# First attention of a two-layer kernel: VectorE's chores dealt anew over the eight head pairs, the choice of experts moved to the fifth pair, each pair's reciprocals taken within the pair

## The reference

```python
h = layernorm(x) * (1 + ca) + sa                     # per batch
q, kv = h @ w_q, h @ w_kv                            # keys and values are one tensor
q, kv = rotary(q) * scale, rotary(kv)
lkv = layernorm_per_head(kv, g, b)                   # local keys and values, windows of 128 and the one before
pkv = softmax(segments_of_16(kv) @ w_proj)           # 16 pooled keys per head
gkv = layernorm_per_head(sum(segments * pkv))
attn = softmax([q @ gkv, q @ lkv] with masks)
x = x + ga * (attn @ [gkv, lkv] @ w_out + b_out)
# then, for layer 0's experts:
h = layernorm(x) * (1 + cb) + sb
top2 = top_k(h @ router_w, 2)                        # two of four experts per token, with softmax weights
```

## Time and profile before

| what | value |
|---|---|
| median of 3 runs | 1521.95 us (1512.76 to 1534.51) |
| the profiled execution's own time | 1513.62 us |
| its span, first to last instruction | 1511.8 us |
| busy, share of the span | PE 79%, DVE 62%, PEld 61%, ACT 54%, POOL 48% |
| mean granted TensorE clock | 0.896 |
| first head pair to last of layer 0's attention | 86.09 to 551.96 us |

### The profile page before, as it was taken

One profiled execution on the slowest core, in us unless ns is written; L12 is line 12 of the kernel. 1 busy time (PEld: TensorE's weight loads), 2 busy tenths in 40 slices (PEclk: granted clock), 3 DMA queues, 4 the chain that ended last, 5 costly groups with the idle time before them and its releaser, 6 DMA issues. The chain is left out here.

```text
span 1511.8 us, 30131 instructions
## 1 busy us (share of the span) xinstructions
PE 1200.5 (79%) x9299; PEld 928.5 (61%) x9299; DVE 931.4 (62%) x2122; ACT 822.3 (54%) x2181; POOL 725.5 (48%) x750
## 2 busy tenths in 40 slices
PE   3368988989889993898899899889937887888436
PEld 1245665656656662898899889889913444444336
DVE  4687787787876533744744664764434677776633
ACT  1256777767677771676676666666612443344101
POOL 2646748567485312565566556556653323211223
PEclk8589999989998995999999999999966999899558
DMA  7500000000000003303003000000063445331145
GB/s 221 174 2 3 1 10 3 8 10 0 9 2 8 10 8 127 124 11 125 8 11 120 16 9 10 12 12 7 10 174 81 84 87 104 58 48 21 23 121 152
DMA packets 152775, 76.43 MB, mean 51 GB/s; under 512 B 99992, under 2 KB 143384, under 8 KB 152408
## 3 DMA queue, kind: packets, MB, share of 16 engines
q1 hardware_dynamic: 144696, 66.42, 16.8%
q0 software_dynamic: 3072, 6.31, 1.3%
q10 hardware_dynamic: 4896, 2.36, 0.5%
HBM read 54.77 MB, written 19.76 MB: 49 GB/s over the span
## 5 line engine op out<-in xcount | busy, mean ns | idle before, releaser
L1477 POOL TENSOR_TENSOR hl<-hid,hh 128x256 fp32r<-128x256 f32 x396 | 294.0, 744 | 218.8 <-ACT hh L1454 215.1
L1520 DVE SCALAR_TENSOR_TENSOR hid<-GU,gub,sg 128x256 f32<-128x256 f32 x396 | 190.5, 482 | 194.7 <-ACT sg L1448 123.5
L1348 PE MATMUL GU<-xh,wh 128*128 128x256 f32 x792 | 233.3, 295 | 39.4 <-DVE wl L1496 30.3
L1448 ACT ACTIVATE sg<-GU,gub 128x256 f32<-128x256 f32 x396 | 188.1, 475 | 123.6 <-PE GU L1350 121.7
L1349 PE MATMUL GU<-xl,wh 128*128 128x256 f32 x792 | 225.3, 284 | 0.0
L1350 PE MATMUL GU<-xh,wl 128*128 128x256 f32 x792 | 225.1, 284 | 0.0
L1348 PEld LDWEIGHTS GU<-xh,wh 128*128 128x128 f32 x792 | 152.1, 192 | 49.0 <-issue 27.3
L1454 ACT CAST hh<-hid 128x256 fp32r<-128x256 f32 x396 | 158.2, 399 | 25.8 <-DVE hid L1520 25.3
L1349 PEld LDWEIGHTS GU<-xl,wh 128*128 128x128 f32 x792 | 152.5, 193 | 0.0
L1350 PEld LDWEIGHTS GU<-xh,wl 128*128 128x128 f32 x792 | 152.2, 192 | 0.0
L648 ACT ACTIVATE prob<-prob,rZ 128x272 f32<-128x272 f32 (+1 forms) x256 | 98.9, 462 | 60.6 <-DVE rZ L1021 55.2
(11 more groups left out here) (312 smaller groups left out, 2842.6 us busy)
## 6 DMA issues: line engine op xcount, KB each, us to landing
raw<-in_expert_w SPq DMA_DIRECT2D x4, 2688.0 KB, 12.0
late<-in_w SPq DMA_DIRECT2D x20, 256.0 KB, 6.1
raw<-in_expert_w SPq DMA_DIRECT2D x4, 1152.0 KB, 6.1
list<-zero SPq DMA_DIRECT2D x4, 1024.0 KB, 8.6
modb<-mod_d SPq DMA_DIRECT2D x9, 384.0 KB, 4.3
early<-rel_d SPq DMA_DIRECT2D x1, 3072.0 KB, 13.1
qkv_d<-qkv SPq DMA_DIRECT2D x48, 64.0 KB
early<-in_w SPq DMA_DIRECT2D x12, 256.0 KB, 4.2
```

The source lines that it names most:

```text
L1348: pe.matmul(out, lhs[0], rhs[0], start=start, stop=False, skip_group_check=True)
L1448: act.activation(sg[:, c % BUFS], GU[c % BUFS][:, 0:TT], ACT.Silu, bias=gub[:, GATE, e * CH0 + c:e * CH0 + c + 1]).then_inc(silu, 1)
L1477: pool.tensor_tensor(hl[:, b], hid[:, b], hh[:, b].bitcast(F32), ALU.subtract).then_inc(hid_lo, 1)
L1520: dve.scalar_tensor_tensor(out=hid[:, c % BUFS], in0=GU[c % BUFS][:, TT:2 * TT], scalar=gub[:, UP, e * CH0 + c:e * CH0 + c + 1], in1=sg[:, ...
```

## The change

Nothing is computed otherwise; the same instructions run, apart from their order.

- Reciprocals of pair n move from the top of pair n+1 into pair n itself, behind the first part of that pair's chores, with the same wait on the pair's own exponentials.
- `kv_center(0)` moves from hp 7 to hp 6, `kv_center(1)` from hp 0 of the next slot to hp 7 of this one. `kv_rotate(0)` moves from hp 6 to hp 5. `kv_cosine(1)` stays in hp 6, `kv_rotate(1)` in hp 7.
- The first sum of squares moves from hp 2 to hp 1; the statistics of layernorm 2 from `residual` at hp 2 to `layernorm2` at hp 3.
- `router_rows` and `choose` move from hp 5 to hp 4, `list_places` from hp 7 to hp 6; with them PE's `router_mm` (hp 5 to 4) and `pos_mm` (hp 7 to 6) and ACT's small exponential (hp 6 to 5). The two banks' orders follow.

The diff; of the ladder that is removed only the head is shown:

```diff
--- before.py
+++ after.py
@@ -312,8 +312,8 @@
         r_step = sem("r_step"); ln2_rstd = sem("ln2_rstd"); n2_done = sem("n2_done"); h2_done = sem("h2_done")
         t_step = sem("t_step"); t_exp = sem("t_exp"); slot_out = sem("slot_out"); kv_rstd = sem("kv_rstd"); g_rstd = sem("g_rstd")
         scat = sem("scat"); count_mm = sem("count_mm"); count_out = sem("count_out")
-        bank0 = Bank(sem("a0_full"), sem("a0_drained"), "lgT:E out:L h2T:L G:E kv00:N kv10:N kT1:E kT3:E pos:L")
-        bank1 = Bank(sem("a1_full"), sem("a1_drained"), "pkT:E hT:N kv01:N router:L kv11:N gkT:E kT0:E kT2:E")
+        bank0 = Bank(sem("a0_full"), sem("a0_drained"), "lgT:E out:L h2T:L G:E kv00:N kv10:N pos:L kT1:E kT3:E")
+        bank1 = Bank(sem("a1_full"), sem("a1_drained"), "pkT:E hT:N router:L kv01:N kv11:N gkT:E kT0:E kT2:E")
         where = {}
         for b, t in ((bank0, A0), (bank1, A1)):
             for name, _ in b.order:
@@ -589,15 +589,17 @@
                         out_mm(slot, slot - 1)
                     if early and hp == 4:
                         G_mm(slot, slot + 1)
-                    if late and hp == 5:
-                        router_mm(slot, slot - 1)
                     if early and hp == 6:
                         gkT_mm(slot, slot + 1)
+                    if late and hp == 6:
+                        pos_mm(slot, slot - 1)
                     if early and hp == 7:
                         for c in (2, 3):
                             kT_mm(slot, slot + 1, np_, c)
                     if (late if hp < 2 else heads):
                         av(n - 2, slot if hp > 1 else slot - 1, bp if hp > 1 else np_, (hp - 2) % HP)
+                    if late and hp == 4:
+                        router_mm(slot, slot - 1)
                     if last:
                         pT_tr(n - 1, (hp - 1) % HP)
                     if early and hp == 0:
@@ -610,8 +612,6 @@
                     if early and hp == 6:
                         for c in (0, 1):
                             kT_mm(slot, slot + 1, np_, c)
-                    if late and hp == 7:
-                        pos_mm(slot, slot - 1)
 
             over_slots(pe, slot_program)
 
@@ -725,7 +725,7 @@
                     if early and hp == 4:
                         bank0.wait_emptied(act, "G", slot)
                         act.activation(gsq[:], gc[:], ACT.Square).then_inc(g_sq, 1)
-                    if late and hp == 6:
+                    if late and hp == 5:
                         act.wait_ge(t_step, T_STEPS * l + 4)
                         act.activation(ew[:, 1, :], ew[:, 0, :], ACT.Exp).then_inc(t_exp, 1)
                     if early and hp == 6:
@@ -836,12 +836,14 @@
                                          scalar=-1.0 / DH0, in1=heads_of(kvr[:, t, :]), op0=ALU.mult,
                                          op1=ALU.add).then_inc(kv_c, 1)
 
+            def kv_squares(b, t):
+                if t == 0 and not known_zero(b):
+                    dve.wait_ge(kv_ss, 3 * b)
+                dve.wait_ge(kv_sq, 2 * b + t + 1)
+                dve.tensor_reduce(ssq[:, t, :], heads_of(kvs[:, t, :]), X, ALU.add).then_inc(kv_ss, 1)
+
             def kv_variance(b):
-                if not known_zero(b):
-                    dve.wait_ge(kv_ss, 3 * b)
-                for t in range(TILES):
-                    dve.wait_ge(kv_sq, 2 * b + t + 1)
-                    dve.tensor_reduce(ssq[:, t, :], heads_of(kvs[:, t, :]), X, ALU.add).then_inc(kv_ss, 1)
+                kv_squares(b, 1)
                 dve.wait_ge(kv_ss, 3 * b + 2)
                 dve.tensor_scalar(krs[:], ssq[:], 1.0 / DH0, EPS, ALU.mult, ALU.add).then_inc(kv_ss, 1)
 
@@ -923,6 +925,8 @@
                 dve.tensor_tensor(res[:], res[:], mods(b, MGA), ALU.mult).then_inc(r_step, 1)
                 dve.wait_ge(r_step, R_STEPS * b + 1)
                 dve.tensor_tensor(rows(x1, b), rows(xt, b), res[:], ALU.add).then_inc(r_step, 1)
+
+            def layernorm2(b):
                 dve.wait_ge(r_step, R_STEPS * b + 2)
                 take_waits(dve, taken)
                 for t in range(TILES):
@@ -1012,13 +1016,14 @@
                 b, l, r = slot + 1, slot - 1, slot + 2
                 for hp in range(HP):
                     n = slot * HP + hp
-                    last = heads if hp > 0 else late
-                    m, pb = n - 1, (hp - 1) % 2
-                    if last:
-                        dve.wait_ge(s_exp, 4 * (m + 1))
-                        if not (isinstance(m, int) and m < 2):
-                            dve.wait_ge(p_norm, m - 1)
-                        dve.reciprocal(rZ[:, pb], Z[:, pb]).then_inc(z_recip, 1)
+
+                    def reciprocals():
+                        if heads:
+                            dve.wait_ge(s_exp, 4 * (n + 1))
+                            if not (isinstance(n, int) and n < 2):
+                                dve.wait_ge(p_norm, n - 1)
+                            dve.reciprocal(rZ[:, hp % 2], Z[:, hp % 2]).then_inc(z_recip, 1)
+
                     if heads:
                         dve.wait_ge(s_mm, n + 1)
                         for t in (1, 0):
@@ -1030,48 +1035,69 @@
                         dve.wait_ge(w_in, 16 * n_w)
                         dve.wait_ge(modT_mm, 3)
                         dve.tensor_tensor(bout[:], bout[:], O[:, 0:D], ALU.add).then_inc(cast, 1)
-                    if early and hp == 0:
-                        logits(b)
-                        kv_center(b, 1)
...
+                    if hp == 0:
+                        if early:
+                            logits(b)
+                        reciprocals()
+                        if norm and not (isinstance(slot, int) and slot == -2):
+                            layernorm1(r)
+                    if hp == 1:
+                        if early:
+                            segment_softmax(slot, b)
+                            kv_squares(b, 0)
+                        reciprocals()
+                    if hp == 2:
+                        if early:
+                            segment_weights(b)
+                            kv_variance(b)
+                        reciprocals()
+                        if late:
+                            if known_zero(l):
+                                for k in range(2):
+                                    dve.wait_ge(modb_in[k], 16)
+                            residual(slot, l)
+                    if hp == 3:
+                        if early:
+                            weights_back(slot, b)
+                            if known_zero(b):
+                                first_row_share(slot, np_)
+                        if late:
+                            layernorm2(l)
+                        reciprocals()
+                        if norm:
+                            if isinstance(slot, int) and slot == -2:
+                                dve.wait_ge(mod_step, 7)
+                            layernorm1_end(r)
+                    if hp == 4:
+                        reciprocals()
+                        if early:
+                            pooled_norm(slot, b)
+                        if late:
+                            router_rows(slot, l)
+                            choose(slot, l)
+                    if hp == 5:
+                        if early:
+                            pooled_variance(b)
+                        if norm:
+                            kv_cosine(slot, r, 0)
+                        reciprocals()
+                        if norm:
+                            kv_rotate(r, 0)
+                    if hp == 6:
+                        if early:
+                            pooled_keys(slot, b, np_)
+                        if late:
+                            list_places(slot, l)
+                        reciprocals()
+                        if norm:
+                            kv_cosine(slot, r, 1)
+                            kv_center(r, 0)
+                    if hp == 7:
+                        if norm:
+                            kv_rotate(r, 1)
+                        reciprocals()
+                        if norm:
+                            kv_center(r, 1)
 
             def rotate_queries(n, buf):
 
```

More of the change, by code:

```diff
@@ L1032, in slot_program @@
                         dve.tensor_tensor(bout[:], bout[:], O[:, 0:D], ALU.add).then_inc(cast, 1)
-                    if early and hp == 0:
-                        logits(b)
-                        kv_center(b, 1)
-                    if norm and hp == 0 and not (isinstance(slot, int) and slot == -2):
-                        layernorm1(r)
-                    if early and hp == 1:
-                        segment_softmax(slot, b)
-                    if early and hp == 2:
-                        segment_weights(b)
-                        kv_variance(b)
@@ L1043, in slot_program @@
-                    if late and hp == 2:
-                        if known_zero(l):
-                            for k in range(2):
```

(31 more changed lines are left out.)

## The result

The changed kernel takes 1532.7 us (median of 22 runs, 1522.7 to 1545.1) against 1522.8 us of the kernel before beside it: ratio 1.0068, 95% interval 1.0040 to 1.0095. It is slower by some 10 us, where -4 was forecast; 1532.7 lies inside the forecast's range, but the sign was wrong. Its profiled execution has a span of 1524.4 us (before 1511.8) at a mean granted clock of 0.890. From the first head pair's maxima to the last's it takes 480.5 us instead of 464.8.

The account below looks back on a forecast made before the run. Bounds moved by pair: PE and POOL's chain in 4, DVE in 5 and 6, ACT behind DVE in 7. Full slots -7, slot 0 -3, slot 6 +1, ramp +5 gave -4: 1518 us, own range 1507 to 1526, widened to 1490 to 1539.

Parts of the forecast that it names:

- rival (b): Pair 6: PE's new 3 us wait for pooled keys lowers the clock, about +3 per slot; 1540 us, chance 0.15.
- Pair 4, +4.1: Full slots: choice held three times beside POOL's 2.33 us products, so pair 5 begins at 433.2 instead of 429.1.
- late layernorm 2 root: Pair 3 into 4: the root stands on POOL ahead of `weigh`, which begins 0.8 to 0.95 us later.
- Pair 5, -2.1: Full slots: DVE loses the 3.65 us choice and gains `kv_rotate(0)`; length 6.7 for 8.82 us.
- pair 7, -2.0: Full slots: normalising starts at once, `pos_mm` leaves PE, centering waits behind `logit_products(1)`; 6.9 for 8.89 us.
- Pair 6, 0: Full slots: 8.0 us if centering precedes `logit_products(0)`, 10.2 if not; middle 9.1 against 9.10 before.
- Pairs 0 to 3, -1.35: Full slots: pair 0 loses the 1.22 us centering, 6.15 for 7.52; moved statistics in pairs 1 to 3 cost 0.
- Slot 6, +1: No key projection hides the choice in pair 4, costing 6 us; pairs 5, 7 and 0 give back 5.
- Slot 0, -3: No choice to block: earlier sum of squares 1.2, pair 0 1.35, half a microsecond in pairs 5 to 7.
- The ramp, +5: Before the first pair: pooled keys' copies wait behind add and sum, 6.0 us later; between 0 and 6, +5 taken.
- Rival (a): Pair 4: the choice is not held up, its operations slipping between POOL's; -32, 1490 us, chance 0.17.
- Rival (c): Pair 6: centering blocked in every slot, clock unharmed, +1.1 times five; 1523.5 us, chance 0.18.

Follow-up runs that it names:

- e2_stats_back: Changed kernel with layernorm 2's statistics moved back to pair 2; ratio to the kernel before 1.0004.
- e5_cut_after: Changed kernel with POOL's gain product cut to a sixteenth of its columns, so the result differs; 1504 us, pair 4 at 10.5–10.9 us.
- e4_choice_only: Kernel before with only router and choice moved from pair 5 to pair 4; ratio to the kernel before 1.0087.
- e7_places_split: e6_repaired with all of `list_places` but its first operation moved to the head of pair 7; ratio to the kernel before 1.0030.
- e11_split_all: e8_split_repaired with POOL's long products of values and logits in quarters too; ratio to the kernel before 0.9960.
- e1_choice_back: Changed kernel with router and choice of experts put back into pair 5; ratio to the kernel before 1.0121.
- e6_repaired: e2_stats_back with layernorm 1's rows ahead of pair 3's reciprocals and pooled keys ahead of slot -1's rotation; ratio to the kernel before 0.9979.
- e10_split_before: Kernel before with only POOL's gain product issued in quarters, same result; ratio to the kernel before 0.9981.
- e8_split_repaired: e6_repaired with POOL's gain product in quarters, same result; ratio to the kernel before 0.9954, 1515.4 us.

## Why the prediction went wrong, point by point

Two steps failed. The first is the price of a chain of small operations moved beside POOL's long products: three holds were put for the choice in pair 4 and there were four, and the places were put at their old 1.7 us in pair 6 and took 5.1. The second is the granted clock, which the sum put at nothing outside rival (b): pair 0 took the forecast's length in the one full slot in which it ran at 1.00, and in slot 6 a low clock cost some 4.8 us. Over the whole attention the granted clock went from 0.93 to 0.91. What moved the low stretches no run shows. In us over slots 1 to 5:

| term | forecast | measured |
|---|---|---|
| pair 4 | +20.5 | +25.6 |
| pair 5 | -10.5 | -11.2 |
| pair 6 | 0 | +5.5 |
| pair 7 | -10.0 | -11.3 |
| pairs 0 to 3 | -6.75 | +0.6 |

**Pair 4, +4.1: right in kind, +5.0 in size.** (Sizes here are those of slot 5.) The step "if the same three do now, they are let go at 429.2, 431.5" describes what happened, but four were held, not three. The rule under it was too narrow: it took operations with two SBUF inputs, and the first held one is the cast L973, 1.74 us, with a single input; in e2_stats_back `h` (L806) is another. The Trainium skill (SBUF — State Buffer, "Who interferes with whom") lists copy, cast and `tensor_scalar` among the operations that can take the port pair shared with GpSimd when their operands meet certain conditions, and says that the one issued first keeps it for the whole instruction. The 1.74 us cast, the 3.12 us of L806 and the cut of e5_cut_after agree; the prediction drew only the half on two inputs from it. The late layernorm 2 root, put at 0.8 to 0.95 us, shows in the kernel after itself, where `weigh` begins 4.40 us into pair 3 for 3.42 before, and in two runs: pair 4 is 13.6 us with the statistics on time (e4_choice_only), and moving them back gives 1.7 us over pairs 3 and 4 (e2_stats_back), with the earlier sum of squares in it. The forecast's 13.6 held that delay, so the rest of its sum was short by it.

**Pair 5, -2.1, and pair 7, -2.0: right.** 6.87 for 8.82 is -1.95, 6.70 for 8.89 is -2.2. Pair 7 was held at the centering, 2.22 us, behind the logit product, as told.

**Pair 6, 0: +0.8.** The centering was not held, 1.21 us. That says nothing against the order of issue from which 10.2 us were read: the centering came at 459.27, when POOL's logit product had ended at 457.99. The choice of places was held in its stead. VectorE's timeline of the kernel after:

```profile
453.26 1.28 DVE L996 TENSOR_TENSOR hotpos<-hot,pos 128x8 f32<-128x8 f32 x2
...
454.66 1.04 DVE L1002 TENSOR_SCALAR ew<-ew 128x2 f32<-128x2 f32 x1
...
456.14 1.87 DVE L1008 CAST slot_now<-slotf 128x4 uint32<-128x4 f32 x1
...
458.15 1.19 DVE L818 TENSOR_TENSOR kvr<-kvraw,const 128x1024 f32<-128x1024 f32 x1
459.27 1.21 DVE L835 SCALAR_TENSOR_TENSOR kvc<-mean,kvr 128x1024 f32<-128x1024 f32 x1
```

The places were costed at 1.7 us, about their time in pair 7 of the kernel before, where POOL had nothing to do beside them; they took 5.1 (453.08 to 458.1). Put back beside an idle POOL in e7_places_split, the same cast took 0.17 us. This is the same slip as with the cast: a chain of small operations was moved next to POOL's long ones and priced at its old duration.

**Pairs 0 to 3, -1.35: -0.4 and +0.6.** This is the largest miss of the full slots, 7.3 us of 16. Pair 0 of slot 3 (slot 5's stands above), and the scores that end it in slot 5:

```profile
275.09:281.33 6.24, 4.27 (x34) 2.80 (x33) 5.22 (x13) 5.45 (x18) 4.59 (x5) 1.00 0.13 45
```

```profile
408.18 1.94 PE L498 MATMUL S<-kT,qr 64*128 64x272 f32 x10
```

At a granted clock of 1.00 pair 0 took 6.24 us, as priced (6.15). In the other four full slots it ran at 0.58 to 0.85 and took 7.14 to 8.39: in slot 5 the low clock lies on the scores behind the logits, 1.94 us for 1.07, for which the maxima then wait. The chain of VectorE was rightly priced, and the clock on TensorE's part of it put at nothing. In the kernel before the pair ran at 0.61 to 0.91, but VectorE, busy for 6.4 to 6.5 us of it, was what ended it in four slots of five and covered the clock. Pair 1 is 5.50 us for 4.88 at 0.88.

By these terms slot 5 is 5.0 - 2.0 + 0.8 - 2.2 - 0.4 + 0.6 = +1.8 us, and the five slots come to +9.2 where -7 was forecast. That is 16 of the 21 us by which the last head pair came later than forecast (+17.3 for -4).

**Slot 6, +1: +6.7.** The choice cost 5.15 us in pair 4 (6 forecast), and pairs 5, 7 and 0 gave back 5.0 as told. Pair 6 is what was missing. TensorE's timeline of the kernel after, and the windows of pairs 5 and 6 of slot 6:

```profile
508.40 0.75 PE L493 MATMUL S<-maskb,identb 128*128 128x288 bf16 x2 [3.46 <-ACT prob L638]
```

```profile
505.31:511.06 5.75, 2.66 (x13) 1.86 (x13) 2.78 (x9) 4.54 (x16) 2.77 (x4) 0.65 0.00 0
511.06:522.98 11.92, 11.92 (x55) 9.48 (x56) 3.93 (x19) 5.62 (x17) 6.37 (x8) 0.60 0.10 30
```

The maxima of pair 5 came late because the choice was held, the exponentials later, and TensorE stood for 3.46 us. The granted clock then was 0.60 through pair 6, all of whose 11.92 us TensorE is busy; the pair took 5.43 us before. The wait alone does not account for the clock. TensorE's wait and the window of pair 6 in slot 6 of e11_split_all:

```profile
489.89 0.74 PE L493 MATMUL S<-maskb,identb 128*128 128x288 bf16 x2 [3.45 <-ACT prob L638]
```

```profile
492.54:499.64 7.10, 7.10 (x53) 5.79 (x53) 4.13 (x18) 4.32 (x14) 3.84 (x6) 0.95 0.06 14
```

There the same wait, at the same place, is followed by a clock of 0.95 and 7.10 us; and in e1_choice_back the pair took 9.05 us at 0.62 without such a wait in pair 5. So some 4.8 us of the slot's loss (11.92 less 7.10) are the low clock's, and why it lasted so long here stays open; without them slot 6 is +1.9 for +1. A low clock behind a wait is what rival (b) had in mind, but in another pair of other slots. In the full slots its own place did show a 1.74 us wait for the pooled keys (3 forecast) and a clock of 0.83 in pair 6, but VectorE was busy for 9.52 of those 9.90 us, so it set nothing.

**Slot 0, -3: +0.3.** Its pair 0 took 7.73 us in every kernel of this study, so the 1.35 us put for it never came. Its pair 4 took 13.97 us for 12.74, and that goes with the clock: over all kernels it took 11.6 to 12.7 us at a granted clock of 0.85 to 0.87, 13.4 to 14.2 at 0.75 or 0.76, and 15.2 to 15.4 at 0.66 or 0.67, with the same 57 matmul records each time. What sets the clock there stays open. **The ramp, +5: about +1.7.** The copies came behind add and sum, as told, 4.3 us later (75.52 for 71.19) where 6.0 was put, but the first maxima only 1.6; e6_repaired, with the old order, has them at 86.04. A good half was hidden. (The first maxima scatter: e10_split_before, with the old ramp, had them at 87.31.) The two together are +1.9 for +2, which is luck: each missed by over 3 us, in opposite directions. **Slot 7, 0: -0.5.**

**The sum.** 1.6 + 0.3 + 9.2 + 6.7 - 0.5 = +17.3 us at the last pair, of which 12.6 are left in the span: in this one execution the later phases took less. Rival (a) is refuted by the four holds. Rival (c) gave 1523.5 by holding the centering; its +1.1 us for pair 6 is what the pair took on average, but the places were held and not the centering.

## What to carry to other kernels

Before a chain of small VectorE operations is moved, look at what GpSimd runs at its new place: each operation there, casts and single-input ones too, can cost the rest of a GpSimd instruction, so price the chain by holds and not by its old duration. If it must stand there, cut the long GpSimd product into a few pieces and measure, since more pieces also mean more holds, and a start 0.07 us later can add two of them. And follow every microsecond of slack that is won to the next stretch that TensorE fills alone; a low clock that falls there takes it back.

## What the runs showed of the hardware

A cast of 128x4 took 0.17 us with GpSimd doing short work, and 1.74 and 2.27 us beside a GpSimd product of 128x1024. In the kernel after, one small VectorE operation passed in some 0.15 us after each release before the next was held; beside products of 128x256 five operations in a row were held in slot 3 of e8_split_repaired. A GpSimd product of 128x1024 took 2.33 us, four of 128x256 some 2.76 (5.51 for eight), so the cut itself costs 0.43 us. The same stretch of TensorE's work took 4.84 us at a granted clock of 1.00 and 8.00 at 0.58. The same wait of TensorE, 3.45 and 3.46 us, was followed by a stretch at 0.95 in one kernel and at 0.60 in another.
